# Pre-norm attention layer on one core: who issues the c transfers, and how finely the first output tile waits

## The chip, the core and the metric

The kernel runs on one core of a Trainium2 chip. The core has TensorE (PE, products), VectorE (DVE), ScalarE (ACT), GpSimd (POOL) and the sync engine (SP). Each runs its own instructions in order and waits for the others by semaphores; SP only waits and issues transfers. The metric is the device time of one execution in microseconds, lower is better.

## The reference

For each of 16 graphs of 512 nodes with 512 features: layer norm without weights, ReLU, 16-head attention under the adjacency mask, output projection and residual.

```
h = jnp.maximum(_layernorm(x, axis=-1), 0.0)
q = heads(h @ Wq + bq); k = heads(h @ Wk + bk); v = heads(h @ Wv + bv)
scores = jnp.einsum('bhqd,bhkd->bhqk', q, k) * scale
scores = jnp.where(mask[:, None] == 0, -jnp.inf, scores)
attn = jax.nn.softmax(scores, axis=-1)
x = x + (attn @ v) @ Wo + bo
```

## The kernel before

**Tiling.** A batch is one graph. The 16 heads go in four head groups g of four heads j. Queries and keys go in tiles of 128. Every projection is made of three products with operands split into a high and a low part (`w_hi`, `w_lo`, `hT_hi`, `hT_lo`, `oT_hi`, `oT_lo`), on four pieces kt of the inner dimension; an output tile's piece kt is head group kt of `oT`.

**Blocks and slots.** The program is a chain of blocks k = 0 to 17 with 64 slots u each, written out by `step(k, parity)` on every engine. Constants at the top fix the slot of everything. In slot u PE makes one score product of pass 1 (L797), one of pass 2 (L811, for some heads with a mask product L814), one kt of a projection tile T = u // 4 (L700 to L702), and in every fourth slot a value product into `psO` (L831). Block k projects q, k, v of batch k, and in its first 16 slots the four output tiles of batch k - 2 (`TILES`); pass 1 of a batch starts at slot 35, pass 2 at slot 60.

**The two passes.** Pass 1 computes the scores with queries on partitions. DVE adds the mask and takes the row maximum (L592), ScalarE takes the exponential and its sum (L430). After a head group DVE forms c from maximum and log-sum (`form_c`, L528 to L533), in a high and a low part. PE turns them (L758), DVE copies them to `c_rows` (L551; slots 8, 24, 40 and 56 for groups 1, 2, 3 and, of the next batch, 0), and two transfers (`load_c`, L388) put them into two extra rows of `q_stack`. Pass 2 computes the scores again, transposed and with c as part of the product, so its exponential (L470) is the softmax itself; for six of eight heads DVE masks it (L599). The first product of pass 2 of a head group waits for `c_in`; the groups start at slots 60, 12, 28 and 44.

**Stacks.** The q and k tiles leave PSUM as a high part (ScalarE, L454) and a low part (DVE, L634) and go by 12 transfers a tile into `q_stack` and `k_stack` (`load_stack`, L223, in the pieces hi0, lo, hi1 of four transfers each).

**The output.** `psO` of a head group leaves as `oT_hi` (ScalarE, L444) and `oT_lo` (DVE, L613); group 3 of batch k - 2 does so in slot 63 of block k - 1, right before block k begins with output tile 0. GpSimd adds bo to a y tile (L343, it waits for the tile's load, L265), DVE adds the output tile (L626), SP stores it (L272). In the last batch GpSimd's adds also wait for the last `c_parts`.

**Queues.** SP issues in this order within a slot: x, adjacency, store of y, load of y, stack. Nothing behind a waiting SP instruction goes out before it. The c transfers are issued by ScalarE, one slot after DVE's copy. In SP's queue load_y for slots 44 and 46 follows the k and q stacks; in the block after the last batch's projections it has no stack before it. PE keeps three banks for pass 1 (`bank1`, `wait_bank1`) and two for projections. `due(n)` is n, at least 0; `have(b)` is true for an existing batch.

## Time and profile before

| | us |
|---|---|
| median of 3 runs | 1709.16 |
| lowest, highest | 1708.68, 1709.55 |
| the profiled execution | 1711.46 |
| its span, first to last instruction | 1709.7 |
| PE busy | 1655.3 (97%) |
| DVE busy | 1527.0 (89%) |
| ACT busy | 1477.9 (86%) |
| POOL busy | 153.1 (9%) |

### The profile page before, as it was taken

The page shows a single profiled execution, that of the slowest core. Times are in us where ns is not written, and L with a number is a line of the kernel's source. Part 1 is how long each engine was busy: PE and PEld are TensorE (multiplying, and loading weights), DVE is VectorE, ACT ScalarE, POOL GpSimd, SP SyncE. Part 2 cuts the span into 40 slices and gives each one's busy share as a digit, 9 for nine tenths or more (in the row PEclk, how much of TensorE's full clock was granted, in tenths as well). Part 3 has the DMA queues.
Part 4 walks back from the last instruction along what each step waited for, and adds up shares of the span by engine and source line. Part 5 has one row for each costly group of instructions (what it writes and reads, how often), then busy time and mean ns, then how long its engine had stood idle before and what let it go on. Part 6 is the DMA issues. An engine that isn't in the chain of part 4 may idle for free.

```text
span 1709.7 us, 27479 instructions
## 1 busy us (share of the span) xinstructions
PE 1655.3 (97%) x7876; PEld 1035.4 (61%) x8001; DVE 1527.0 (89%) x3656; ACT 1477.9 (86%) x3498; POOL 153.1 (9%) x203
## 2 busy tenths in 40 slices
PE   6899999999999999999999999999999999999997
PEld 5556666666666666666665666666666666666653
DVE  4799998989989899998999989899998999989895
ACT  3799898898888989899898988989899888989985
POOL 2001100001010011100011000111100001000001
PEclk9799999999999999999999999999999999999998
DMA  6433343333433334343333433344343433433320
GB/s 198 107 86 100 106 111 90 113 90 110 116 95 108 88 113 109 100 108 89 114 92 109 114 92 106 93 118 111 102 106 86 112 96 106 114 97 94 92 85 26
DMA packets 117166, 175.18 MB, mean 102 GB/s; under 512 B 30860, under 2 KB 32920, under 8 KB 117016
## 3 DMA queue, kind: packets, MB, share of 16 engines
q1 hardware_dynamic: 112536, 171.83, 37.3%
q10 hardware_dynamic: 4480, 1.58, 0.4%
q8 instruction: 66, 1.08, 0.3%
q14 instruction: 84, 0.69, 0.1%
HBM read 54.79 MB, written 16.78 MB: 42 GB/s over the span
## 4 chain that ended last, share of the span: by engine, by line
PE 78%; DVE 15%; issue 3%; ACT 2%; SPq 1%; DMA 0%; DVEq 0%; ACTq 0%
PE ps L797 14%; PE psO L831 13%; PE psP L700 13%; PE psP L701 11%; PE ps L811 11%; PE psP L702 11%; DVE ps L592 5%; DVE probs L599 4%; PE ps L814 2%; PE ps L747 1%; DVE x_tile L513 1%; DVE stats L505 1%; ACT ps L430 1%; DVE y_tile L626 1%; DVE oT_lo L613 1%
## 5 line engine op out<-in xcount | busy, mean ns | idle before, releaser
L592 DVE CUSTOM_DVE_ANT_0 ps<-ps,bias_q 128x512 f32<-128x512 f32 x1024 | 708.7, 694 | 132.5 <-PE ps L797 122.4
L430 ACT ACTIVATE ps<-ps,neg_max 128x512 f32<-128x512 f32 x1024 | 686.9, 671 | 92.1 <-DVE neg_max L592 75.6
L470 ACT ACTIVATE probs<-ps 128x512 f32<-128x512 f32 x1024 | 622.5, 608 | 72.0 <-PE ps L814 37.7
L599 DVE SCALAR_TENSOR_TENSOR probs<-bias_k,probs 128x512 f32<-128x512 bf16 x768 | 552.9, 721 | 8.2 <-ACT probs L470 8.1
L797 PE MATMUL ps<-k_stack,q_stack 96*128 96x512 f32 x1024 | 450.8, 441 | 21.3 <-ACT ps L430 11.5
L811 PE MATMUL ps<-q_stack,k_stack 98*128 98x512 f32 x1024 | 410.0, 401 | 3.2 <-ACT probs L470 3.0
L797 PEld LDWEIGHTS ps<-k_stack,q_stack 96*128 96x128 f32 x1024 | 193.6, 189 | 277.0 <-ACT ps L430 132.2
L831 PE MATMUL psO<-probs,v_sb 128*32 128x512 f32 x2048 | 274.5, 608 | 2.0 <-DVE oT_lo L613 0.9
L811 PEld LDWEIGHTS ps<-q_stack,k_stack 98*128 98x128 f32 x1024 | 194.9, 190 | 40.1 <-ACT probs L470 14.9
L430 ACT ACTIVATION_READ_ACCUMULATOR ps<-ps,neg_max 128x1 f32 x1024 | 218.2, 213 | 0.0
L592 DVE DVE_READ_ACCUMULATOR2_ANT neg_max<- 128x1 f32 x1024 | 144.0, 141 | 0.0
L343 POOL TENSOR_TENSOR y_tile<-y_tile,bo_row 128x512 f32<-128x512 f32 x62 | 84.8, 1367 | 412.0 <-DMA y_tile<-in_x_dram 384.7
L700 PE MATMUL psP<-wo_hi,oT_hi 128*128 128x512 f32 x248 | 111.8, 451 | 9.3 <-DVE oT_lo L613 9.3
L329 POOL TENSOR_SCALAR mean_var<-mean_var 128x1 f32<-128x1 f32 x64 | 20.7, 323 | 1108.5 <-DVE mean_var L508 1108.4
L700 PE MATMUL psP<-wv_hi,hT_hi 128*128 128x512 f32 x256 | 114.1, 446 | 0.8 <-DVE hT_lo L544 0.8
L700 PE MATMUL psP<-hT_hi,wq_hi 128*128 128x512 f32 x256 | 114.4, 447 | 0.2 <-DVE hT_lo L544 0.2
L700 PE MATMUL psP<-hT_hi,wk_hi 128*128 128x512 f32 x256 | 113.2, 442 | 0.4 <-DVE wk_lo L556 0.3
L701 PE MATMUL psP<-hT_lo,wq_hi 128*128 128x512 f32 x256 | 102.8, 402 | 0.0
L701 PE MATMUL psP<-wv_lo,hT_hi 128*128 128x512 f32 x256 | 102.2, 399 | 0.0
L702 PE MATMUL psP<-hT_hi,wq_lo 128*128 128x512 f32 x256 | 102.0, 399 | 0.0
L702 PE MATMUL psP<-wv_hi,hT_lo 128*128 128x512 f32 x256 | 101.7, 397 | 0.0
L701 PE MATMUL psP<-hT_lo,wk_hi 128*128 128x512 f32 x256 | 101.6, 397 | 0.0
(75 smaller groups left out, 1882.2 us busy)
## 6 DMA issues: line engine op xcount, KB each, us to landing
q_stack<-part_hi SPq DMA_DIRECT2D x512, 64.0 KB, 2.0
k_stack<-part_hi SPq DMA_DIRECT2D x504, 64.0 KB, 2.0
x_tile<-in_x_dram SPq DMA_DIRECT2D x64, 256.0 KB, 2.9
y_tile<-in_x_dram SPq DMA_DIRECT2D x64, 256.0 KB, 2.9
adj_tile<-in_adj_dram SPq DMA_DIRECT2D x64, 256.0 KB, 3.0
q_stack<-part_lo SPq DMA_DIRECT2D x256, 64.0 KB, 2.0
k_stack<-part_lo SPq DMA_DIRECT2D x256, 64.0 KB, 2.0
out_dram<-y_tile SPq DMA_DIRECT2D x62, 256.0 KB, 2.1
```

The costliest lines, as they stand in the source:

```text
L343: nc.gpsimd.tensor_tensor(y_view(b, t), y_view(b, t), bo_row[:], ALU.add).then_inc(y_plus_bo, 1)
L430: nc.scalar.activation(item, item, ACT.Exp, scale=-1.0, bias=neg_max[:, g % 2, col:col + 1], accum_out=exp_sum[:, col:col + 1]).then_inc(e ...
L470: nc.scalar.activation(probs[:, n % P_RING, :], ps2[:, n % 2, :], ACT.Exp, scale=SCALE).then_inc(exp2_done, 1)
L592: nc.vector.tensor_tensor_reduce(bank1(("s", u)), bank1(("s", u)), bias_q[:, qt, :], -SCALE, 3.0e38, ALU.add, ALU.min, neg_max[:, g % 2, c ...
L599: nc.vector.scalar_tensor_tensor(out=probs[:, n % P_RING, :], in0=bias_k[:, n % 16 // 4, :], scalar=-MASKED, in1=probs[:, n % P_RING, :], ...
L700: nc.tensor.matmul(acc, w_h, m_h, start=(kt == 0), stop=False)
L701: nc.tensor.matmul(acc, w_h, m_l, start=False, stop=False)
L702: return nc.tensor.matmul(acc, w_l, m_h, start=False, stop=(kt == NT - 1))
L797: nc.tensor.matmul(bank1(("s", u)), q_stack[0:STACK, g, j, P * qt:P * qt + P], k_stack[0:STACK, g, j, :], start=True, stop=True).then_inc( ...
L811: last = nc.tensor.matmul(ps2[:, n % 2, :], k_stack[:, g, j, P * kt:P * kt + P], q_stack[:, g, j, :], start=True, stop=(n % 8 in VECTOR_MA ...
L814: last = nc.tensor.matmul(ps2[:, n % 2, :], ident_b[:], bias_k[:, kt, :], start=False, stop=True)
L831: last = nc.tensor.matmul(psO[32 * j:32 * j + 32, :], v_sb[:, 1 - parity, kt, at:at + DH], probs[:, (4 * n + j) % P_RING, :], start=(kt == ...
```

## The change

The c transfers go from ScalarE's queue to SP's, but for the first pair of all. In SP's order they stand in slot 9 (group 1, after the store of an output tile), slot 25 (group 2, after an adjacency load and before a k stack), slot 37 (group 3, inside the k stack, after its pieces hi0 and lo) and slot 57 (group 0). The first output tile's wait for all four head groups of `oT` becomes one wait before each kt, for that group.

```diff
--- before.py
+++ after.py
@@ -223,6 +223,14 @@
                     queue.dma_start(stack[row:row + 32, g, j, :].bitcast(F32),
                                     part[32 * j:32 * j + 32, i % 2, :].bitcast(F32)).then_inc(stack_in[kind], 16)
 
+        def load_c(queue, b, g):
+
+            if have(b):
+                queue.wait_ge(c_rows_done, due(4 * b + g + 1))
+                for part in range(2):
+                    queue.dma_start(q_stack[STACK + part:STACK + part + 1, g, :, :].rearrange("a j (t q) -> a (j t) q", q=P).bitcast(F32),
+                                    c_rows[16 * part:16 * part + 16, :].bitcast(F32)).then_inc(c_in, 16)
+
         def halves(b, g):
 
             return [slice(0, S // 2), slice(S // 2, S)] if (b, g) == (LAST, NT - 1) else [slice(0, S)]
@@ -288,10 +296,20 @@
                     if u in (7, 11) and k - 2 != LAST: load_y(k - 2, (u + 1) // 4)
                     if u in (44, 46): load_y(k - 1, (u - 44) // 2)
                     if u in (48, 50) and k - 1 == LAST: load_y(LAST, (u - 44) // 2)
+                    if u == 9: load_c(sp, k - 1, 1)
+                    if u == 25: load_c(sp, k - 1, 2)
+                    if u == 57 and k > 0: load_c(sp, k, 0)
+                    if u == 37 and not tile_at(k, 8): load_c(sp, k - 1, 3)
                     if u % 4 == 1:
                         done = tile_at(k, u // 4 - 1) if u >= 4 else tile_at(k - 1, 15)
                         if done and done[0] in "qk" and done != ("k", 0, 0):
-                            load_stack(sp, done[2], QK_ORDER.index(done[:2]))
+                            i = QK_ORDER.index(done[:2])
+                            if u == 37:
+                                load_stack(sp, done[2], i, ("hi0", "lo"))
+                                load_c(sp, k - 1, 3)
+                                load_stack(sp, done[2], i, ("hi1",))
+                            else:
+                                load_stack(sp, done[2], i)
                         if done == ("k", 0, 0):
                             load_stack(sp, 0, QK_ORDER.index(("k", 0)), ("lo",))
 
@@ -379,14 +397,6 @@
                 kind, n = QK_ORDER[i]
                 if have(k):
                     act.wait_ge(stack_in[kind], due(192 * (4 * k + n + 1)))
-
-            def load_c(b, g):
-
-                if have(b):
-                    act.wait_ge(c_rows_done, due(4 * b + g + 1))
-                    for part in range(2):
-                        act.dma_start(q_stack[STACK + part:STACK + part + 1, g, :, :].rearrange("a j (t q) -> a (j t) q", q=P).bitcast(F32),
-                                      c_rows[16 * part:16 * part + 16, :].bitcast(F32)).then_inc(c_in, 16)
 
             nc.scalar.preload_act_table_set("natural_log_exp_and_others")
 
@@ -471,7 +481,7 @@
                                              ).then_inc(exp2_done, 1)
                     for kind, n, rel in TURNS.get(u - 1, ()):
                         if kind == "c":
-                            load_c(k + rel, n)
+                            if (k + rel, n) == (0, 0): load_c(act, 0, 0)
                     for kind, n, rel in TURNS.get(u, ()):
                         if kind == "h" and have(k):
                             act.wait_ge(h_turned, due(4 * k + n + 1))
@@ -709,10 +719,6 @@
                 if kt == 0:
 
                     wait_tile_out(*((k, T - 2) if T >= 2 else (k - 1, T + 14)))
-                    if T == 0:
-
-                        pe.wait_ge(o_hi_done, due(4 * b + 4))
-                        pe.wait_ge(o_lo_done, due(4 * b + 4))
                     if T == 4 or k == 0 and kind == "v":
 
                         pe.wait_ge(h_hi_done, due(4 * b + (4 if T == 4 else n + 1)))
@@ -721,6 +727,10 @@
                         pe.wait_ge(w_lo_done[kind], 1)
                 if k == 0 and n == 0 and kind == "v":
                     pe.wait_ge(w_lo_done["v"], kt + 1)
+                if T == 0 and kind == "o":
+
+                    pe.wait_ge(o_hi_done, due(4 * b + kt + 1))
+                    pe.wait_ge(o_lo_done, due(4 * b + kt + 1))
                 acc = psP[:, T % 2, :]
                 rows = slice(P * n, P * n + P)
                 if kind in "qk":
```

On PE, the start of a block: output tile 0. First before:

```order
L797 MATMUL ps<-k_stack,q_stack 128x512 [waits exp1_done]
L811 MATMUL ps<-q_stack,k_stack 128x512 [waits exp2_done,m_done]
L700 MATMUL psP<-wo_hi,oT_hi 128x512 [waits o_hi_done,o_lo_done,qk_lo_done,qk_hi_done]
L701 MATMUL psP<-wo_lo,oT_hi 128x512
L702 MATMUL psP<-wo_hi,oT_lo 128x512
L797 MATMUL ps<-k_stack,q_stack 128x512 [waits exp1_done]
L811 MATMUL ps<-q_stack,k_stack 128x512 [waits exp2_done]
L700 MATMUL psP<-wo_hi,oT_hi 128x512
L701 MATMUL psP<-wo_lo,oT_hi 128x512
```

and now:

```order
L807 MATMUL ps<-k_stack,q_stack 128x512 [waits exp1_done]
L821 MATMUL ps<-q_stack,k_stack 128x512 [waits exp2_done,m_done]
L710 MATMUL psP<-wo_hi,oT_hi 128x512 [waits o_hi_done,o_lo_done,qk_lo_done,qk_hi_done]
L711 MATMUL psP<-wo_lo,oT_hi 128x512
L712 MATMUL psP<-wo_hi,oT_lo 128x512
L807 MATMUL ps<-k_stack,q_stack 128x512 [waits exp1_done]
L821 MATMUL ps<-q_stack,k_stack 128x512 [waits exp2_done]
L710 MATMUL psP<-wo_hi,oT_hi 128x512 [waits o_lo_done,o_hi_done]
L711 MATMUL psP<-wo_lo,oT_hi 128x512
```

The wait for `o_hi_done` and `o_lo_done` stands before each product L710 of the tile, each with a count of its own (L700 and L710, L797 and L807 are the same lines).

On SP, slots 24 to 25 of a block. Before:

```order
L223 DMA q_stack<-part_hi 32x512 [waits qk_hi_done]
L223 DMA q_stack<-part_hi 32x512 x3
L252 DMA adj_tile<-in_adj_dram 128x512 [waits bias_done]
L223 DMA k_stack<-part_hi 32x512 [waits qk_hi_done,scores2]
L223 DMA k_stack<-part_hi 32x512 x3
L223 DMA k_stack<-part_lo 32x512 [waits qk_lo_done]
L223 DMA k_stack<-part_lo 32x512 x3
```

and now:

```order
L223 DMA q_stack<-part_hi 32x512 [waits qk_hi_done]
L223 DMA q_stack<-part_hi 32x512 x3
L260 DMA adj_tile<-in_adj_dram 128x512 [waits bias_done]
L231 DMA q_stack<-c_rows 1x16x128 [waits c_rows_done]
L231 DMA q_stack<-c_rows 1x16x128
L223 DMA k_stack<-part_hi 32x512 [waits qk_hi_done,scores2]
L223 DMA k_stack<-part_hi 32x512 x3
L223 DMA k_stack<-part_lo 32x512 [waits qk_lo_done]
L223 DMA k_stack<-part_lo 32x512 x3
```

The pair of c stands between the adjacency load and the k stack, and all that follows is two issues later.

On SP, slots 37 to 44. Before:

```order
L223 DMA k_stack<-part_lo 32x512 [waits qk_lo_done]
L223 DMA k_stack<-part_lo 32x512 x3
L223 DMA k_stack<-part_hi 32x512 [waits qk_hi_done]
L223 DMA k_stack<-part_hi 32x512 x3
L265 DMA y_tile<-in_x_dram 128x512 [waits y_out0]
L223 DMA q_stack<-part_hi 32x512 [waits qk_hi_done,scores2]
```

and now:

```order
L223 DMA k_stack<-part_lo 32x512 [waits qk_lo_done]
L223 DMA k_stack<-part_lo 32x512 x3
L231 DMA q_stack<-c_rows 1x16x128 [waits c_rows_done]
L231 DMA q_stack<-c_rows 1x16x128
L223 DMA k_stack<-part_hi 32x512 [waits qk_hi_done,scores2]
L223 DMA k_stack<-part_hi 32x512 x3
L273 DMA y_tile<-in_x_dram 128x512 [waits y_out0]
L223 DMA q_stack<-part_hi 32x512 [waits qk_hi_done,scores2]
```

The pair waits in the middle of the k stack, and the load of y comes behind it.

On SP, the end of the program, from the last batch's c on. Before:

```order
L272 DMA out_dram<-y_tile 128x512 [waits y_done]
L265 DMA y_tile<-in_x_dram 128x512 [waits y_out1]
L272 DMA out_dram<-y_tile 128x512 [waits y_done] x2
L265 DMA y_tile<-in_x_dram 128x512 [waits y_out0]
L265 DMA y_tile<-in_x_dram 128x512 [waits y_out1]
L265 DMA x_tile<-in_x_dram 128x512 [waits h_turned] x2
L272 DMA out_dram<-y_tile 128x512 [waits y_done] x2
```

and now:

```order
L231 DMA q_stack<-c_rows 1x16x128 [waits c_rows_done]
L231 DMA q_stack<-c_rows 1x16x128
L273 DMA y_tile<-in_x_dram 128x512 [waits y_out1]
L280 DMA out_dram<-y_tile 128x512 [waits y_done] x2
L231 DMA q_stack<-c_rows 1x16x128 [waits c_rows_done]
L231 DMA q_stack<-c_rows 1x16x128
L231 DMA q_stack<-c_rows 1x16x128 [waits c_rows_done]
L231 DMA q_stack<-c_rows 1x16x128
L273 DMA y_tile<-in_x_dram 128x512 [waits y_out0]
L273 DMA y_tile<-in_x_dram 128x512 [waits y_out1]
L273 DMA x_tile<-in_x_dram 128x512 [waits h_turned] x2
L280 DMA out_dram<-y_tile 128x512 [waits y_done] x2
```

The four loads of the last y tiles (two of them into `x_tile`) now follow the last pair of c.

## Rows read from the trace of the kernel before

**Rows 1.** Page: busy time by engine; shares of the chain that ended last.

```profile
PE 1655.3 (97%) x7876; PEld 1035.4 (61%) x8001; DVE 1527.0 (89%) x3656; ACT 1477.9 (86%) x3498; POOL 153.1 (9%) x203
...
PE 78%; DVE 15%; issue 3%; ACT 2%; SPq 1%; DMA 0%; DVEq 0%; ACTq 0%
```

**Rows 2.** What PE waited for: us in total, times, longest us.

```profile
PE psP L700 <- DVE oT_lo L613: 9.3, 16, 1.2
```

**Rows 3.** Order of time, a block's first slots: start us, us, engine, line, operation.

```profile
798.26 0.40 PE L797 MATMUL ps<-k_stack,q_stack 96*128 96x512 f32 x1
...
798.49 0.39 PE L811 MATMUL ps<-q_stack,k_stack 98*128 98x512 f32 x1
798.53 0.74 DVE L613 SCALAR_TENSOR_TENSOR oT_lo<-psO,cols,oT_hi 128x512 fp32r<-128x512 f32 x1
...
799.42 0.47 PE L700 MATMUL psP<-wo_hi,oT_hi 128*128 128x512 f32 x1 [0.53 <-DVE oT_lo L613]
...
800.19 0.40 PE L797 MATMUL ps<-k_stack,q_stack 96*128 96x512 f32 x1
...
800.62 0.70 DVE L592 CUSTOM_DVE_ANT_0 ps<-ps,bias_q 128x512 f32<-128x512 f32 x1 [0.69 <-PE ps L797]
...
800.71 0.27 ACT L430 ACTIVATION_READ_ACCUMULATOR ps<-ps,neg_max 128x1 f32 x1
```

**Rows 4.** Order of time, ScalarE, slots 57 and 58 of a block.

```profile
787.38 0.51 ACTq L388 DMA_DIRECT2D q_stack<-c_rows  x1
...
787.93 0.61 ACTq L388 DMA_DIRECT2D q_stack<-c_rows  x1
...
788.59 0.66 ACT L430 ACTIVATE ps<-ps,neg_max 128x512 f32<-128x512 f32 x1 [0.25 <-issue]
```

**Rows 5.** Line 388, the c transfers: who waited (us, times), landing times.

```profile
  PEld ps L811: 0.6, 2
...
DMA to landing us min/median/max: 1.8/1.9/3.4
```

**Rows 6.** Order of time, the sync queue, around slot 25.

```profile
1252.83 0.59 SPq L252 DMA_DIRECT2D adj_tile<-in_adj_dram  x1
1253.51 2.41 SPq L223 DMA_DIRECT2D k_stack<-part_hi  x4
```

**Rows 7.** k_stack transfers issued from 1253.4 to 1254.3: landing times.

```profile
DMA to landing us min/median/max: 2.4/2.4/2.5
```

**Rows 8.** Order of time, PE, slot 28 of the same block.

```profile
1256.32 0.40 PE L811 MATMUL ps<-q_stack,k_stack 98*128 98x512 f32 x1
```

**Rows 9.** Order of time, the sync queue, slots 40 to 44.

```profile
865.60 2.49 SPq L223 DMA_DIRECT2D k_stack<-part_hi  x4
868.13 0.58 SPq L265 DMA_DIRECT2D y_tile<-in_x_dram  x1
```

**Rows 10.** Order of time, GpSimd, slots 46 to 52 of that block.

```profile
871.18 1.62 POOL L343 TENSOR_TENSOR y_tile<-y_tile,bo_row 128x512 f32<-128x512 f32 x1 [2.28 <-DMA y_tile<-in_x_dram]
880.68 1.30 POOL L343 TENSOR_TENSOR y_tile<-y_tile,bo_row 128x512 f32<-128x512 f32 x1 [7.88 <-DMA y_tile<-in_x_dram]
```

**Rows 11.** Order of time, DVE, the same slots.

```profile
872.82 0.69 DVE L599 SCALAR_TENSOR_TENSOR probs<-bias_k,probs 128x512 f32<-128x512 bf16 x1
...
880.85 1.68 DVE L599 SCALAR_TENSOR_TENSOR probs<-bias_k,probs 128x512 f32<-128x512 bf16 x1
```

**Rows 12.** Windows, slots 40 to 56 of two blocks: length, then busy us by engine.

```profile
1379.50:1400.50 21.00, 20.56 (x102) 12.94 (x101) 20.31 (x49) 18.33 (x46) 4.17 (x6) 1.00 0.44 111
1071.10:1091.20 20.10, 20.10 (x101) 13.04 (x101) 19.41 (x50) 18.71 (x45) 4.60 (x6) 1.00 0.46 114
```

**Rows 13.** Order of time, GpSimd, in the last block.

```profile
1673.62 2.98 POOL L343 TENSOR_TENSOR y_tile<-y_tile,bo_row 128x512 f32<-128x512 f32 x2 [27.37 <-DVE c_parts L533]
```

**Rows 14.** Order of time, DVE, in the last block.

```profile
1678.76 0.27 DVE L551 CAST c_rows<-ps 32x128 fp32r<-32x128 f32 x1
...
1683.63 2.00 DVE L599 SCALAR_TENSOR_TENSOR probs<-bias_k,probs 128x512 f32<-128x512 bf16 x3 [1.17 <-ACT probs L470]
1685.93 0.75 DVE L613 SCALAR_TENSOR_TENSOR oT_lo<-psO,cols,oT_hi 128x512 fp32r<-128x512 f32 x1 [0.30 <-ACT oT_hi L444]
```

## Prediction

> **What bounds the kernel now.** I read the page first: TensorE (PE) is busy 97% of the span and holds 78% of the chain that ended last, VectorE (DVE) 15% [rows 1]. PE is near its own pace, so only two things move the time: PE stalls that go and PE stalls that come. I read the list of what PE waited for, then the order of time around each place that the diff touches.
>
> The first place is the first output tile of a block. The list has 16 waits of its first product for `oT_lo`, 9.3 us together, the longest 1.2 [rows 2]; 15 are this tile (the output tiles of batches 0 to 14) and the longest is the one at the end, which the change leaves alone. In the order of time PE starts one product 0.23 us after another (798.26, 798.49), but the first output product comes 0.93 us after the one before it, when DVE has written `oT_lo` [rows 3]. So the stall is 0.93 - 0.23 = 0.70 us of PE's pace, and 0.53 in the idle column only because the ends of products are modelled.
>
> The second place is the scalar queue. A pair of c transfers takes 0.51 + 0.61 us of issue there, and the exponential behind it starts 0.25 us late [rows 4]. PE hardly waits for these transfers: two waits, 0.6 us in all, of 64 pairs, both at the end of the kernel [rows 5].
>
> **The sum, part by part**, made against the profiled execution (span 1709.7, time 1711.46, of which 1.8 lie around the span and stay). The median of the runs shown is 1709.16, 2.3 lower; the forecast is for such a median, so the sum is put on 1709.16.
>
> *Waits per head group: -10.3 us.* At kt 0, 1 and 2 the products need head groups that were ready long before; only kt 3 needs the late one, and before it stands the value product of slot 2, which waits for the same `oT_lo`. PE gets there about two slots later, while DVE ends `oT_lo` at 798.53 + 0.74 = 799.27 [rows 3], so the wait is over. What is late next? The score product now at 800.19 moves to 799.49 and needs a bank whose exponential is done by then; the one after it moves to about 801.0 and needs the exponential that ends at 800.71 + 0.27 = 800.98 [rows 3]. Both just fit; I take off 0.02 to 0.1. DVE follows: before its next reduction it idles 0.69 us waiting for that very product [rows 3], so DVE, which is full over the next ten slots, also starts 0.7 earlier and does not take the gain back. 15 x 0.69 = 10.3; bounds 9 and 10.8 (0.6 and 0.72 a batch).
>
> *Issues taken from ScalarE: -0.3 us.* 63 of 64 pairs go, 63 x 1.12 = 71 us of issue. In the steady part the late exponential is covered: PE has three score banks, keeps starting products at its pace and DVE is behind anyway. Only in the last block, where ScalarE is on the chain for some slots, do two pairs count; 0 to 1 us, I take 0.3.
>
> *c for head group 2 behind the adjacency load: +1.7 us.* In the sync (SP) queue the pair comes behind a whole q stack and an adjacency load. In a typical batch that load is issued at 1252.83 and the first k piece at 1253.51 [rows 6]. The c pair takes the place of the first two k pieces, so its second transfer goes out at about 1254.1. Alone it would land 1.9 us later [rows 5], at 1256.0; the two k pieces that stand there now land after 2.4 us [rows 7], which gives 1256.5. The product that needs c starts at 1256.32 [rows 8]. So 0.3 us early by one row and 0.2 late by the other. I take 0.11 a batch, nearer to the k pieces, as they are in the same queue behind the same load, but are larger: 15 x 0.11 = 1.7; bounds 0 and 0.23 x 15 = 3.5, since any lateness here is straight on PE's path. So a transfer right behind this load lands 0.5 us later than one on the other queue. The Trainium skill ("DMA: Bandwidth & Descriptors", Queues, rings and completion order) says that scalar and sync queue own a ring each on the same engines, that an engine takes turns between rings but works through one ring in order. The trace agrees so far as the 2.4 shows. The rule speaks against the change: by it the pair lands with the load's data, like the k pieces, and the term is near 3.5 rather than 0.
>
> *c for head groups 1 and 3 and 0: +0.8 us.* Group 0 is issued into an idle SP queue, earlier than now. Group 3 stands after eight pieces of a k stack, about when its rows are ready. Group 1 must now follow the wait for an output tile and its store. Landings scatter by 1.6 us (1.8 to 3.4 [rows 5]), so a few may be late; group 1 is followed by slots in which PE waits for DVE anyway, which covers most of it. 0 to 3, I take 0.8.
>
> *The y load behind the k stack: +5 us.* All that is queued behind the pair moves back. The adjacency load after the k stack of group 2 has slack. But at slot 37 the pair sits inside a k stack, and behind it, with no gap, comes the load of a y tile (the last four pieces at 865.60, the load at 868.13 [rows 9]); it goes out 0.51 + 0.61 us [rows 4] to 1.25 us (two of the pieces, four of which take 2.49 [rows 9]) later, say 1.2, and so does GpSimd's add of bo, which waits for it (now 871.18 [rows 10]). That add and DVE's masking step (L599) exclude each other: where the add at 880.68 [rows 10] runs, the mask started at 880.85 takes 1.68 us and ends 0.55 after the add, where none runs (872.82) it takes 0.69 [rows 11]. Today the first add falls on steps of DVE that do not care. At 871.18 + 1.2 = 872.4 it runs until 873.7, and the mask at 872.82 must wait: 873.7 + 0.55 - 873.5 = 0.7 us lost. How much reaches PE? In a batch where both adds hit (masks 1.1 and 0.6 us too long) the stretch has 21.00 - 20.56 = 0.44 us of PE idle (0.9 by the starts of its products, an estimate), in one where only the second hit, none [rows 12]. So DVE has some 0.65 us to spare, and the second add uses that up already. Placed against the start of slot 46, the first add begins in 11 of the 15 blocks, that of [rows 10] among them, where 1.2 us later is worse by some 0.6, and in four, that of the first stretch of [rows 12] among them, where it is better (there it hits now) by some 0.4; both are my estimates from the same reckoning. 11 x 0.6 - 4 x 0.4 = 5; bounds 0 and 8. The Trainium skill ("SBUF — State Buffer", SBUF: two separate sides) states such a lock between the two engines for a step with two SBUF inputs; the trace agrees (1.68 against 0.69).
>
> *The end: +2.5 us.* The last batch's four y loads stand in SP's queue behind the last c pair. Now they are long there and GpSimd adds at 1673.62, as soon as `c_parts` is done [rows 13], in slots where PE has other work. After, they go out only when the c rows are copied (1678.76 + 0.27 [rows 14]) and the pair is issued: 1680.2, landing by about 1683.2, and four adds run until about 1690. In that time the masks of the last heads start at 1683.63 (three in 2.00 us) and `oT_lo` at 1685.93 [rows 14]. Each mask would wait for an add, one in about 1.7 us (two take 2.98, the first of them 1.3 as in [rows 10]): three end at 1688.5 instead of 1685.63, `oT_lo` is 2.5 us late, and PE's next output product waits for it. Bounds 1 and 3.5.
>
> Sum: -10.3 - 0.3 + 1.7 + 0.8 + 5 + 2.5 = -0.6. From 1709.16: **1708.6 us**.
>
> **The rivals.**
> *The gain stays* (faster). For it: the removed stall is read directly, 15 times; the y load's new place depends on when loads land, and 0.5 us less would put the add where it costs nothing. Against: the adds that do hit. With the 5 as 0, c of group 2 at 0.5 and the other groups at 0.6: -10.3 - 0.3 + 0.5 + 0.6 + 2.5 = -7.0, 1702.
> *The adds hit the masks* (slower). The same mechanism as in the sum, behind the y load of slot 44, at its full price: the first add makes a mask 1.1 us too long in every block, the second 0.6, together 1.7, less the spare 0.65 about 1.05, where the blocks lose some 0.3 today: 15 x 0.75 = 11 instead of 5, and c of group 2 at 3.5 instead of 1.7. -0.6 + 6 + 1.8 = +7.2, 1716. It decides when the new stalls of the blocks pass (10.3 + 0.3 - 2.5 + 3.4) / 15 = 0.77 us each; the sum has (1.7 + 0.8 + 5) / 15 = 0.5. For it speaks that the add's place is set by a landing time, against it that a block in which the add is free exists for every delay.
> *The head-group wait only moves* (slower or same). If the score product two further on must wait for the exponential that I put 0.02 us ahead of it, a part of the 0.7 stays: at a gain of 0.3 a block, 4.5 in place of 10.3, the sum is +5.2, 1714. The rows leave little room for it, since DVE's idle 0.69 goes too.
>
> **How the numbers follow.** A measurement of this kernel can tell 0.2%, 3.4 us. Likeliest is that gain and new stalls balance: 0.43, within 3.4 us of 1709.2. Gain stays: 0.34. Adds at full price: 0.16; wait moves: 0.07. Faster 0.34, same 0.43, slower 0.23. The likeliest case alone spans 1705.8 to 1712.5; the range takes in most of the first rival and part of the second: 1701 to 1714.
>
> **What would show it.** Right: the wait of the first output product for `oT_lo` gone from PE's list but for the one at the end; DMA issues of c under SP; GpSimd's first add about 1.2 us later after slot 46, with masks of over 1.2 us there; the last four adds around 1683 to 1690 instead of 1673 to 1680; PE waits for `q_stack<-c_rows` at group 2. Wrong: a wait of equal size at the score product of slot 1 or 2; or a y load that lands where no mask stands, with the time some 7 us down.

## The result

Over 22 runs each the changed kernel takes 1712.9 us at the median (1709.1 to 1718.8), the kernel before 1710.3: **ratio 1.0018, 95% interval 1.0010 to 1.0026**. The forecast was 1708.6, that is 0.03% faster. So it is slower by about 3 us. The median lies inside the range of 1701 to 1714 and 0.4 us above the 1705.8 to 1712.5 of the likeliest case, and the interval leaves out both "no change" and "faster". The unedited changed kernel, run again beside some of the experiments on another chip, gave 0.9997 (0.9984 to 1.0011), which can't be told from no change. Both comparisons weighted by their widths put the change at +0.13%, 2.1 us, and that is what the steps are held against below.

The profiled execution of the changed kernel has a span of 1710.4 us. Its page, busy time by engine and the shares of the chain that ended last (compare [rows 1]):

```profile
PE 1659.1 (97%) x7876; PEld 1035.2 (61%) x8001; DVE 1530.9 (90%) x3656; ACT 1471.2 (86%) x3498; POOL 153.1 (9%) x203
...
PE 73%; DVE 15%; issue 4%; ACT 4%; SPq 2%; DMA 1%; another core or an unknown queue 0%; DVEq 0%; ACTq 0%
```

The page hardly differs. The list of what PE waited for does (us in total, times, longest us; compare [rows 2]):

```profile
PE psP L710 <- DVE oT_lo L623: 3.6, 2, 2.4
PE ps L821 <- DMA q_stack<-c_rows: 2.2, 4, 0.9
```

Sixteen waits for `oT_lo` have become two: the one of 1.2 us that was always at the end, and a new one of 2.4. And PE now waits for c. The product that follows the wait of [rows 3] stood 0.93 us behind its predecessor; in the same block of the changed kernel, PE's order of time (start us, us, engine, line, operation):

```profile
795.99 0.40 PE L821 MATMUL ps<-q_stack,k_stack 98*128 98x512 f32 x1
...
796.22 0.40 PE L710 MATMUL psP<-wo_hi,oT_hi 128*128 128x512 f32 x1
```

It now comes 0.23 us behind. So the stall that the change aimed at is gone, and the time came back elsewhere. To see where, I cut the traces at PE's score products of pass 1, four slots at a time, and summed each stretch over blocks 1 to 15. Worked out from those starts, changed kernel less the kernel before, in us (first and second profiled execution):

| stretch | 1st | 2nd | forecast |
|---|---|---|---|
| slots 0 to 3, 15 blocks | -9.5 | -9.4 | -10.3 with block 16 |
| slots 28 to 31 | +2.9 | +2.0 | +1.7 |
| slots 48 to 55 | +5.5 | +8.2 | +5 |
| slots 12 to 15 | -0.3 | +1.9 | part of +0.8 |
| slots 44 to 47 and 60 to 63 | 0 | +0.2 | part of +0.8 |
| all other slots of blocks 1 to 15 | -0.5 | -0.8 | 0 |
| ahead of block 1 | -1.1 | -1.5 | 0 |
| block 16, up to the last score product of pass 1 | +1.1 | +2.0 | part of -10.3 |
| behind that product (the tail) | +2.6 | +0.1 | +2.5 |
| sum (span) | +0.8 | +2.7 | |

Of block 16, -0.2 is the wait. Most of the rest comes in the slots in which TensorE is granted half its clock (1.2 GHz) for 3.4 us (first profile, from 1648.0) and for 6.8 us (second). Before's profile has no such stretch there; eight of the 14 profiles of the study have one, that of "delay only" below among them, which moves neither c nor the waits. Ahead of block 1 every other profile is shorter than before's too, by 0.3 to 2.0 us, so that row says nothing of the change.

### The profile page after: what moved, and what is told of

It reads as the page before. It is cut to its first block, busy times and chain, and to the rows that moved or that the text cites. A ratio compares the mean times of both kernels' runs of the same rounds, so it can differ in the third digit from the quotient of the medians.

```text
span 1710.4 us, 27540 instructions
## 1 busy us (share of the span) xinstructions
PE 1659.1 (97%) x7876; PEld 1035.2 (61%) x8001; DVE 1530.9 (90%) x3656; ACT 1471.2 (86%) x3498; POOL 153.1 (9%) x203
## 4 chain that ended last, share of the span: by engine, by line
PE 73%; DVE 15%; issue 4%; ACT 4%; SPq 2%; DMA 1%; another core or an unknown queue 0%; DVEq 0%; ACTq 0%
PE ps L807 14%; PE psO L841 12%; PE psP L710 12%; PE ps L821 11%; PE psP L711 11%; PE psP L712 10%; DVE ps L602 5%; DVE probs L609 4%; ACT ps L440 2%; PE ps L824 1%; SPq L223 1%; PE ps L757 1%; DVE x_tile L523 1%; ACT probs L480 1%; DVE stats L515 1%
## 5 line engine op out<-in xcount | busy, mean ns | idle before, releaser
L807 PE MATMUL ps<-k_stack,q_stack 96*128 96x512 f32 x1024 | 451.6, 441 | 21.4 <-ACT ps L440 11.5
L807 PEld LDWEIGHTS ps<-k_stack,q_stack 96*128 96x128 f32 x1024 | 194.0, 189 | 280.2 <-ACT ps L440 113.7
L440 ACT ACTIVATION_READ_ACCUMULATOR ps<-ps,neg_max 128x1 f32 x1024 | 222.7, 217 | 0.0
L710 PE MATMUL psP<-wo_hi,oT_hi 128*128 128x512 f32 x248 | 111.9, 451 | 3.6 <-DVE oT_lo L623 3.6
L710 PE MATMUL psP<-wv_hi,hT_hi 128*128 128x512 f32 x256 | 113.7, 444 | 0.9 <-DVE hT_lo L554 0.8
L710 PE MATMUL psP<-hT_hi,wq_hi 128*128 128x512 f32 x256 | 114.0, 445 | 0.2 <-DVE hT_lo L554 0.2
L710 PE MATMUL psP<-hT_hi,wk_hi 128*128 128x512 f32 x256 | 113.3, 443 | 0.3 <-DVE wk_lo L566 0.3
```

Source lines behind the costliest of these rows:

```text
L440: nc.scalar.activation(item, item, ACT.Exp, scale=-1.0, bias=neg_max[:, g % 2, col:col + 1], accum_out=exp_sum[:, col:col + 1]).then_inc(e ...
L710: nc.tensor.matmul(acc, w_h, m_h, start=(kt == 0), stop=False)
L807: nc.tensor.matmul(bank1(("s", u)), q_stack[0:STACK, g, j, P * qt:P * qt + P], k_stack[0:STACK, g, j, :], start=True, stop=True).then_inc( ...
```

## The experiments

Where a run is called so many us faster or slower than the kernel before, that is its ratio less 1, times 1711; the changed kernel counts as 2.1 us slower. With 6 to 12 runs of each kernel such a figure is good to 2 to 4 us. The table at the end has the stretches of all of them, each from one profile.

### The two halves of the change alone

```diff
 # kernel before, c on the scalar queue
-                    if T == 0:
-                        pe.wait_ge(o_hi_done, due(4 * b + 4))
-                        pe.wait_ge(o_lo_done, due(4 * b + 4))
...
+                if T == 0 and kind == "o":
+                    pe.wait_ge(o_hi_done, due(4 * b + kt + 1))
+                    pe.wait_ge(o_lo_done, due(4 * b + kt + 1))
```

> One part of the change alone: the first output tile waits per head group, and all c pairs stay on the scalar queue. Theory 'ledger' (the wait's gain is cancelled by costs of the c transfers on the sync queue): the stretch of slots 0 to 3 is 9.5 us shorter over the 15 blocks in the changed kernel's trace and nothing else moves here, so 9.5 us faster than the kernel before, ratio 0.9944 (0.9935 to 0.9955). The tensor engine's waits for DVE's oT_lo at a block's start are gone, and the stretch of slots 48 to 55 has its old length. Rival 'idle time moves' (the tensor engine comes earlier to the next group of slots and waits there for ScalarE or for a mask, so the gain is handed back whatever queue carries c): ratio 0.999 to 1.001, with the other groups of slots longer by 9 us in sum.

Measured 0.993 (0.9910 to 0.9951), 12 us faster. The rival falls: slots 0 to 3 are 9.0 us shorter, and the other stretches take back 2.4 at most (slots 12 to 15 and 48 to 55).

```diff
 # changed kernel, the two edits of the wait undone
-                if T == 0 and kind == "o":
-                    pe.wait_ge(o_hi_done, due(4 * b + kt + 1))
-                    pe.wait_ge(o_lo_done, due(4 * b + kt + 1))
...
+                    if T == 0:
+                        pe.wait_ge(o_hi_done, due(4 * b + 4))
+                        pe.wait_ge(o_lo_done, due(4 * b + 4))
```

> The other part alone: all c pairs but the first on the sync queue, the old wait at slot 0 kept. Ledger: +2.9 us at slots 28 to 31, +5.5 us at slots 48 to 55, +2.6 us in the tail, together 11 us slower than the kernel before, ratio 1.0064; up to 1.0075 if the further stretch at half clock in the last block (1.6 us) comes with it. Rival 'not additive' (the later c pairs and y loads are late only because the block starts 0.65 us earlier, so without the new wait they hit nothing): ratio 1.000 to 1.003.

Measured 1.0061 (1.0042 to 1.0080), 10 us slower, with +3.9 in slots 28 to 31 and +6.2 in slots 48 to 55. The rival "not additive" falls. The halves add up to -2 us, within some 5 us by their intervals, so they agree with the whole (+2.1); the change is a gain and a loss of about one size, not two edits that do nothing.

### The changed kernel once more

> The changed kernel once more, unedited, so that its variants stand beside it on one chip, and for a second profiled execution of it. The sums by groups of slots should repeat: slots 0 to 3 shorter by 9.0 to 9.5 us over the 15 blocks, slots 28 to 31 longer by 2.9 us, slots 48 to 55 by 5.5 us (4 to 7). The stretches of TensorE at half clock in the last block and the tail (five in the first profiled execution, 1648 us on) are the open point. Theory 'the clock comes with the kernel': four or five stretches again, a tail behind the last score product of 43 us, ratio 1.001 to 1.003. Rival 'the clock is drawn by lot': three stretches or fewer, a tail of 39 to 41.5 us, and the same ratio all the same, since the sum over many executions holds both.

Ratio 0.9997; sums in the table above. It has three stretches at half clock in the last block and the tail instead of five, and a tail of 40.5 us. That is what the second theory, the lot, said; the one stretch that does come with the kernel is looked at under "The end".

### Head group 3's pair, and the y load behind it

```diff
 # changed kernel; group 3's pair issued by the scalar queue
-                    if u == 37 and not tile_at(k, 8): load_c(sp, k - 1, 3)
...
-                                load_stack(sp, done[2], i, ("hi0", "lo"))
-                                load_c(sp, k - 1, 3)
-                                load_stack(sp, done[2], i, ("hi1",))
+                                load_stack(sp, done[2], i)
```

> The changed kernel with head group 3's pair back on the scalar queue and the k stack of slot 37 issued in one piece again; the other groups stay on the sync queue. Ledger: y loads of slots 44 and 46 go out 1.2 us earlier again, the GpSimd adds end before DVE's masks, slots 48 to 55 lose 5.5 us, and the last batch's y loads stand behind one pair less, which gives back up to 2.6 us in the tail: 6 to 8 us faster than the changed kernel, so 3.5 to 5.5 us faster than the kernel before, ratio 0.997 to 0.998. Rival 'the adds are not the cause' (slots 48 to 55 grew because the block's start moved against the ScalarE or because of the k stack's last piece): slots 48 to 55 keep at least 4 of the 5.5 us and the ratio is 1.000 to 1.002.

Measured 0.9959 (0.9943 to 0.9975), 7 us faster than before and 9 faster than the changed kernel. That is more than the 3.5 to 5.5 us expected, though slots 48 to 55 keep +3.0 of 5.5 to 8.2, where the theory had nothing left and the rival at least 4. The difference lies in the tail, which has its shortest length, 36.7. Slots 28 to 31, with group 2's pair still on the sync queue, keep +2.8.

The opposite test puts only the delay into the kernel before:

```diff
 # kernel before; pad is a tile that nobody reads, c stays on the scalar queue
+                            if u == 37 and k > 0:
+                                load_stack(sp, done[2], i, ("hi0", "lo"))
+                                sp.wait_ge(pad_in, 32 * (k - 1))
+                                for part in range(2):
+                                    sp.dma_start(pad[16 * part:16 * part + 16, :], ident[16 * part:16 * part + 16, :]).then_inc(pad_in, 16)
+                                load_stack(sp, done[2], i, ("hi1",))
```

> The kernel before, with nothing of the change: only two small transfers (8 KB each, into a tile that nobody reads) on the sync queue at the place in the k stack of slot 37 where the changed kernel has its c pair. It tests the delay of the y loads by itself, with c on the scalar queue and the old waits. Theory 'the adds meet the masks': the first GpSimd add starts at slot 46 plus 0.9 to 2 us instead of slot 45/46 plus 0.9 us, slots 48 to 55 grow by 5 to 8 us over the 15 blocks (5.5 and 8.2 in the two profiles of the changed kernel) and nothing else does; ratio 1.003 to 1.005. Rival 'the delay is harmless, what costs is c's own lateness': slots 48 to 55 within 1.5 us of the kernel before, ratio 0.999 to 1.001.

Measured 1.0029 (1.0014 to 1.0043), 5 us slower. Two transfers that nobody waits for cost time, because of what stands behind them. The sync queue of this kernel, then GpSimd and DVE some 3 us later, in order of time:

```profile
1077.30 1.22 SPq L301 DMA_DIRECT2D pad<-ident  x2
1078.62 2.44 SPq L225 DMA_DIRECT2D k_stack<-part_hi  x4
1081.10 0.58 SPq L267 DMA_DIRECT2D y_tile<-in_x_dram  x1
```

```profile
1084.15 1.27 POOL L353 TENSOR_TENSOR y_tile<-y_tile,bo_row 128x512 f32<-128x512 f32 x1 [3.44 <-DMA y_tile<-in_x_dram]
1092.61 1.35 POOL L353 TENSOR_TENSOR y_tile<-y_tile,bo_row 128x512 f32<-128x512 f32 x1 [7.19 <-DMA y_tile<-in_x_dram]
```

```profile
1084.04 0.69 DVE L602 CUSTOM_DVE_ANT_0 ps<-ps,bias_q 128x512 f32<-128x512 f32 x1
...
1084.64 1.33 DVE L609 SCALAR_TENSOR_TENSOR probs<-bias_k,probs 128x512 f32<-128x512 bf16 x1
```

The y load goes out at 1081.10, the add runs from 1084.15 to 1085.42, and the mask that starts in it (1084.64) ends 0.55 after it: 1.33 us instead of 0.69. The reduction at 1084.04, which reads PSUM, overlaps the add and keeps its 0.69. Slots 48 to 55 grow by 3.2, less than the 5 to 8 expected. Slots 12 to 15, which the edit doesn't touch, grew by 5.3 in this profile. I have no reason for that: the masks of slots 6 to 15 are lengthened by adds as much as before (11.9 us in all against 12.1, worked out as in the next paragraph). So a stretch of a single profile is good to a few us only.

The masks of all 14 profiles show the lock and its price. Each profile has over 700 masks that no add overlaps, and none of them takes more than 0.70 us; the 53 to 65 that an add overlaps take 0.9 to 1.2 in the median and up to 1.83. What the masks of slots 46 to 55 take above 0.70 us each, summed over 15 blocks, follows the place of the y loads: 5.5 to 9.0 us in the five kernels with the loads in their old place (5.8 before), 10.3 to 14.7 in the seven that delay them (14.7 and 13.4 in the changed kernel, 11.4 here), and nothing in the two kernels below that load y early. The first add starts 0.37 us after the start of slot 46 before (median of the blocks), 1.34 and 1.69 in the changed kernel, and 1.39 here.

The third test leaves every pair where the change has it and moves the y loads:

```diff
 # changed kernel
-                    if u in (44, 46): load_y(k - 1, (u - 44) // 2)
+                    if u in (44, 46) and k - 1 == LAST: load_y(k - 1, (u - 44) // 2)
+                    if u == 36 and k - 1 != LAST:
+                        for t in range(2): load_y(k - 1, t)
```

> The changed kernel with the y loads of slots 44 and 46 issued at slot 36, ahead of the k stack and its c pair; nothing taken back. Theory 'the adds meet the masks' (the y load behind the c pair makes the GpSimd add start 1.2 us later, which lengthens DVE's masks and so the scores): the adds start at slot 44 or 45, slots 48 to 51 give back their 3.1 us, slots 52 to 55 at least 1.5 of their 2.4 us unless the first add's new place stretches another mask, in sum 3 to 5.5 us faster than the changed kernel, ratio 0.9985 to 1.0000. Rival 'it is the score products of slots 48 to 55 that wait for stacks, not for masks': ratio and slots as in the changed kernel (1.0018, +5.5 us). Rival 'the add just moves onto another mask': slots 40 to 47 grow by what slots 48 to 55 lose, ratio 1.001 to 1.002.

Ratio 1.0006 (0.9995 to 1.0016): nothing won, and none of the three theories has it right. Slots 48 to 55 are 3.6 us shorter than even before, their masks free of adds. But slots 44 to 47 grew by 7.8, and not through a mask. The sync queue, and PE's weight load of the product that needs the pair:

```profile
1474.85 0.58 SPq L260 DMA_DIRECT2D adj_tile<-in_adj_dram  x1
1475.47 0.93 SPq L273 DMA_DIRECT2D y_tile<-in_x_dram  x2
1476.50 2.41 SPq L223 DMA_DIRECT2D k_stack<-part_hi  x4
```

```profile
1485.84 0.19 PEld L823 LDWEIGHTS ps<-q_stack,k_stack 98*128 98x128 f32 x1 [1.58 <-DMA q_stack<-c_rows]
```

From slot 33 on the queue has no gap, so two loads put in ahead make group 3's pair, whose margin in the first profile of the changed kernel was 0.4 to 1.6 us, late for 13 of 16 batches (PE's weight loads waited 28 times for c, 18.4 us, against 10 times and 5.4 us). A part of the 3.6 us can be DVE and ScalarE catching up while PE waited for c, for without that wait the same move shortens slots 48 to 55 by less. With c on the scalar queue the move is free:

```diff
 # kernel with the waits alone
-                    if u in (44, 46): load_y(k - 1, (u - 44) // 2)
+                    if u in (44, 46) and k - 1 == LAST: load_y(k - 1, (u - 44) // 2)
+                    if u == 36 and k - 1 != LAST:
+                        for t in range(2): load_y(k - 1, t)
```

> The waits per head group with all c pairs on the scalar queue (as in the run of that part alone, ratio 0.993), and the y loads of slots 44 and 46 issued at slot 36. If the adds that meet masks also cost the kernel before something: slots 48 to 55 take 196.2 us in it over 15 blocks, and without any lengthened mask 4 x 6.11 x ... is not known, so bounded by the wait lists: the blocks with the least take 12.3 us for the eight slots, which gives 185 us for 15, so up to 4 us more than the first part alone can be had, ratio 0.991 to 0.993. Rival 'the add moves onto another mask': 0.993 to 0.995.

Measured 0.9944 (0.9930 to 0.9958). Slots 48 to 55 are at -0.2, slots 44 to 47 at 0. That is 1.7 us better in the profile than the waits alone, and not to be told from it by the ratios. It is also hardly better than the kernel before, whose masks were 5.8 us longer; unless the moved waits cost something there, so much lengthening costs PE little.

### Head group 2's pair

```diff
 # changed kernel; group 2's pair issued by the scalar queue
-                    if u == 25: load_c(sp, k - 1, 2)
```

> The changed kernel with head group 2's pair back on the scalar queue, so that it is not behind the adj load and the q stack on the sync queue. Theory 'the queue makes it late': slots 28 to 31 go back to 6.11 us a block, 2.9 us in all, the tensor engine's waits for that pair go (longest margin again 1.9 us), 2.9 us faster than the changed kernel, ratio to the kernel before about 1.000. Rival 'the pair is not what is late' (it is the q stack ahead of it that a slow issue holds up, whoever carries the pair): slots 28 to 31 keep 2 us or more, ratio 1.0013 to 1.0018.

Measured 0.9991 (0.9975 to 1.0007), 1.5 us faster than before and 3.6 faster than the changed kernel; slots 28 to 31 are back at 6.11 us in every block. So the pair is what was late, and the rival falls. The second test keeps it on the sync queue and changes what is ahead of it:

```diff
 # changed kernel; ADJ_AT[1] is slot 24, where its load is taken out
+                    if u == 25:
+                        load_c(sp, k - 1, 2)
+                        load_adj(k, 1)
```

> The changed kernel with the adj load of slot 24 issued behind head group 2's pair instead of ahead of it; all pairs stay on the sync queue. Theory 'the term of head group 2 is the queue ahead of it': the pair goes out 0.63 us earlier, its margin goes from 0.04 to 0.3 us to about 0.8 us, which covers all but the issues that take 1.2 us or more, so slots 28 to 31 give back 2 to 2.9 us over the 15 blocks, ratio 0.001 to 0.0015 below the changed kernel's. Rival 'the adj load is then what comes late' (DVE turns it into the mask bias two slots later): slots 28 to 39 grow by 1 us or more and nothing is won.

Measured 0.9981 (0.9966 to 0.9996). Slots 28 to 31: +0.2 instead of +2.0 to 2.9; slots 32 to 39 don't grow, so the adj load is not late. In the changed kernel the product came 0.04 to 0.23 us after its pair had landed (blocks 1 to 15), and 0.04 means that it had waited for it, as it did in five of the 15 blocks. Now the distance is about 1.0: the pair goes out 0.63 earlier and lands faster. Behind the load its second transfer mostly took 2.0 to 2.5 us to land, ahead of it 1.84 to 1.95. One pair of the changed kernel, then one of this kernel, from issue to landing:

```profile
DMA to landing us min/median/max: 2.2/2.3/2.4
```

```profile
DMA to landing us min/median/max: 1.8/1.8/1.8
```

The Trainium skill ("DMA: Bandwidth & Descriptors", Queues, rings and completion order) says that each of the engines works through one queue's ring in order; both numbers agree with it.

What the prediction missed is the shape of this loss. In 12 of the 15 blocks of the first profile the stretch is at most 0.13 us longer; three blocks hold 2.8 of the 2.9. The sync queue in one of them, and PE:

```profile
1449.70 2.49 SPq L223 DMA_DIRECT2D q_stack<-part_lo  x4
1452.23 3.60 SPq L223 DMA_DIRECT2D q_stack<-part_hi  x4
1455.88 0.58 SPq L260 DMA_DIRECT2D adj_tile<-in_adj_dram  x1
1456.50 1.15 SPq L231 DMA_DIRECT2D q_stack<-c_rows  x2
```

```profile
1459.33 0.50 PE L821 MATMUL ps<-q_stack,k_stack 98*128 98x512 f32 x1 [0.93 <-DMA q_stack<-c_rows]
```

Four issues take 2.49 us, these four 3.60, and everything behind them is 1.1 late. The kernel before has such issues too (34 of its 1536 stack issues take over 0.9 us, up to 2.2), one of them inside this row of its sync queue:

```profile
862.35 3.20 SPq L223 DMA_DIRECT2D k_stack<-part_lo  x4
```

There the stacks had slack for it, and c was on the other queue.

### The end

```diff
 # changed kernel
+                    if u in (44, 46) and k - 1 != LAST: load_y(k - 1, (u - 44) // 2)
+                    if u == 18 and k - 1 == LAST:
+                        for t in range(NT): load_y(LAST, t)
```

> The changed kernel, with one step moved: in the last block the four y loads are issued ahead of the last two c pairs (at slot 18) and no longer behind them. Ledger: the tail after the last score product is 2.6 us shorter, all else as in the changed kernel: 2.6 us faster than it, ratio to the kernel before 1.0000 (0.9993 to 1.0008). If the half-clock stretches in the last block go as well, 1.6 us more. Rival 'the clock makes the tail long' (the tail's growth is TensorE at half clock, which comes whatever the y loads do): the ratio stays at 1.0015 to 1.002 and the tail at 43 us.

Measured 0.9978 (0.9964 to 0.9991), 3.8 us faster than before and 5.9 faster than the changed kernel, where 2.6 was expected. The tail is 36.7 us instead of 43.0 and 40.5. In the changed kernel GpSimd, DVE and PE near its end:

```profile
1681.61 2.97 POOL L361 TENSOR_TENSOR y_tile<-y_tile,bo_row 128x512 f32<-128x512 f32 x2 [40.33 <-DMA y_tile<-in_x_dram]
1684.55 3.39 POOL L361 TENSOR_TENSOR x_tile<-x_tile,bo_row 128x512 f32<-128x512 f32 x2
```

```profile
1681.84 4.97 DVE L609 SCALAR_TENSOR_TENSOR probs<-bias_k,probs 128x512 f32<-128x512 bf16 x3 [1.46 <-ACT probs L480]
1686.73 0.74 DVE L623 SCALAR_TENSOR_TENSOR oT_lo<-psO,cols,oT_hi 128x512 fp32r<-128x512 f32 x1
```

```profile
1687.62 0.47 PE L710 MATMUL psP<-wo_hi,oT_hi 128*128 128x512 f32 x1 [2.42 <-DVE oT_lo L623]
```

Four adds from 1681.61 to 1687.94, three masks in 4.97 us instead of 2.00 [rows 14], and PE 2.42 us idle. Windows of the same stretch (length, busy us by engine, then TensorE's granted clock):

```profile
1685.20:1688.90 3.70, 1.28 (x9) 0.83 (x12) 3.70 (x4) 0.68 (x2) 2.74 (x2) 1.00 0.00 0
1688.90:1692.40 3.50, 3.50 (x12) 1.41 (x6) 0.88 (x2) 1.11 (x2) 0.00 (x0) 0.51 0.00 0
```

The windows of this experiment at the same distance (17.8 us on) from its last score product of pass 1; its adds ran from 1673.81:

```profile
1687.24:1690.94 3.70, 3.70 (x20) 1.85 (x19) 1.44 (x3) 1.90 (x4) 0.00 (x0) 1.00 0.00 0
1690.94:1694.44 3.50, 3.30 (x17) 1.44 (x16) 1.82 (x3) 1.94 (x4) 0.00 (x0) 1.00 0.02 5
```

From 1.3 us after the idle 2.42 us TensorE is granted 1.2 GHz for 3.4 us, and does 12 products; the other kernel, at 2.4 GHz throughout, does 17 in its window. Of six profiles with the late adds (both of the changed kernel and four experiments) all have the stall, 2.1 to 2.4 us; in four the clock falls 0.9 to 1.4 us after it, in one just before it ends, in one not. Of the eight with early adds none has the stall, and none a fall at that place. Their tails are 42.4 us in the mean (40.5 to 43.5) against 38.6 (36.7 to 41.1). So the end costs 3.8, not 2.5. Before's own tail, 40.4, is one of the long ones of its kind, which is why the first table has less. An idle stretch alone doesn't decide the clock: in before's profile PE is idle for 1.5 of the 4 us from 1648, and the clock stays.

### What a pair costs where nothing stands behind it, and both places mended

```diff
 # changed kernel; only group 0's pair (slot 57) stays on the sync queue
-                            if (k + rel, n) == (0, 0): load_c(act, 0, 0)
+                            if (k + rel, n) == (0, 0) or n == 1 or n == 2 or n == 3: load_c(act, k + rel, n)
```

> The waits per head group, with only head group 0's pair on the sync queue (it lands 3.4 us ahead of its need there, 2.1 us on the scalar queue) and the other three pairs back on the scalar queue. Theory 'a pair costs only what it pushes': at slot 57 nothing is queued close behind it, so the time is that of the waits alone, ratio 0.993 (0.991 to 0.995), slots 48 to 63 as in that run. Rival 'each pair on the sync queue costs a quarter of the loss' (12 us less for the waits, about 12 to 14 us back for four pairs): 3 us more, ratio 0.995 to 0.996, with slots 0 to 3 or 60 to 63 longer.

Measured 0.9939 (0.9916 to 0.9962), which can't be told from the time of the waits alone. Slots 48 to 63 are as in that run. A pair in a gap of the sync queue costs nothing that these runs can show.

```diff
 # changed kernel with both: group 3's pair on the scalar queue, adj behind group 2's
+                    if u == 25:
+                        load_c(sp, k - 1, 2)
+                        load_adj(k, 1)
...
+                            if (k + rel, n) == (0, 0) or n == 3: load_c(act, k + rel, n)
```

> The changed kernel with both costs of the sync queue taken away at once: head group 3's pair back on the scalar queue (k stack of slot 37 in one piece), and the adj load of slot 24 behind head group 2's pair. Groups 0, 1 and 2 stay on the sync queue, the waits per head group stay. Theory 'two places hold the whole loss' (the pair in the k stack with the y loads behind it, and the adj load ahead of group 2's pair): the gain of the waits stands alone, ratio 0.993 to 0.995; slots 28 to 31 and 48 to 55 together within 2.5 us of the kernel before, and the tail's adds start right behind the last slots. Rival 'the gain can't be had with pairs on the sync queue' (group 1's pair with its margin of 0.04 to 0.3 us is next, or issues on the sync queue get slower with it): ratio 0.996 or more, with slots 12 to 15 longer by 4 us or more.

Measured 0.9939 (0.9918 to 0.9960). With three of four pairs still on the sync queue the gain of the waits stands alone. So two places held the whole loss, to the 3.6 us that the interval allows: the pair inside the k stack, with the y loads behind it in the blocks and at the end, and the adj load ahead of group 2's pair. Four kernels (this one, "waits only", "y early, waits" and "group 0 sync", 0.9930 to 0.9944) can't be told apart; the simplest is the waits alone.

Stretches of all kernels in us against the kernel before (15 blocks each, worked out from the starts of PE's score products of pass 1), and the tail's own length. "Late" marks kernels whose last y loads stand behind the last c pair:

| kernel | 0-3 | 12-15 | 28-31 | 44-47 | 48-55 | tail | ratio |
|---|---|---|---|---|---|---|---|
| before | 0 | 0 | 0 | 0 | 0 | 40.4 | 1 |
| changed, 1st | -9.5 | -0.3 | +2.9 | 0 | +5.5 | 43.0 late | 1.0018 |
| changed, 2nd | -9.4 | +1.9 | +2.0 | +0.2 | +8.2 | 40.5 late | 0.9997 |
| waits only | -9.0 | +0.9 | 0 | 0 | +1.5 | 38.9 | 0.9930 |
| c on sync only | 0 | +1.4 | +3.9 | +1.2 | +6.2 | 41.4 late | 1.0061 |
| group 3 scalar | -9.0 | +3.9 | +2.8 | 0 | +3.0 | 36.7 | 0.9959 |
| last y first | -9.0 | 0 | +3.2 | 0 | +7.0 | 36.7 | 0.9978 |
| group 2 scalar | -9.4 | +2.5 | 0 | 0 | +2.1 | 42.9 late | 0.9991 |
| delay only | 0 | +5.3 | 0 | 0 | +3.2 | 41.1 | 1.0029 |
| y early, changed | -9.5 | -0.1 | +4.9 | +7.8 | -3.6 | 42.8 late | 1.0006 |
| y early, waits | -9.4 | +1.9 | 0 | 0 | -0.2 | 38.7 | 0.9944 |
| group 0 sync | -9.4 | +1.2 | 0 | 0 | +1.7 | 37.3 | 0.9939 |
| adj behind pair | -9.4 | +0.7 | +0.2 | 0 | +3.4 | 43.5 late | 0.9981 |
| both mended | -9.1 | +2.6 | 0 | 0 | +1.8 | 38.9 | 0.9939 |

## Why the prediction was wrong

The mechanisms were right, each at its place, and a balance near zero came out. But the sum said slightly faster and the kernel is slightly slower: -0.6 against +2.1 us. The steps that failed are three terms that were too kind: the count of the waits (by 0.6), the c pair of group 2 (by 0.8) and the end (by 1.3). A forecast of -0.6 from terms with bounds of several us could not tell the sign; that the sum came within 3 us is partly luck, since the term of the y load, the second largest, can't be pinned.

- **Waits per head group, -10.3: measured -9.7.** The price of one was right (0.67 of 0.69 us). The count was not: one of the 15 is in block 16, where ScalarE sets the pace, and gives back 0.21 only. 14 blocks make 9.5.
- **Issues taken from ScalarE, -0.3:** nothing to be seen of it. PE's longest list, score products that waited for exponentials, is 11.5 us before, 11.5 and 13.8 after.
- **Group 2's pair, +1.7: +2.0 and +2.9.** The place, the queue and the landing behind the load (2.4 forecast, mostly 2.0 to 2.5 measured) were right. The step that failed is "0.11 a batch": lateness was read from one typical batch of [rows 6]. A typical batch loses nothing, and a pair that is just punctual loses in the rare slow issues ahead of it, which only the spread of the issue times shows.
- **Groups 1, 3 and 0, +0.8:** near nothing. Group 1's product starts 0.04 to 0.33 us after its pair has landed, and in three or four blocks it waited; yet slots 12 to 15 have -0.3 to +3.9 us in the nine profiles with that pair on the sync queue and 0 to +5.3 in the five with it on the scalar queue.
- **The y load behind the k stack, +5: +5.5 and +8.2.** The mechanism is shown by the delay alone and by the masks of all profiles. The size can't be pinned: kernels that delay the load have +2.1 to +8.2, the four with the load in its old place and the waits moved have +1.5 to +3.0, though the profile of before, the base of it all, has 0. I take before's profile for a draw that is short by about 2.0, which makes the term 6.9 - 2.0 = 4.9. That is argued and not shown: all four have the waits moved, and an earlier start of the blocks could cost the 2.0 itself. Against that speaks that with the load delayed two kernels with the old wait have +3.2 and +6.2 and five profiles with the new one +2.1 to +8.2. That 4.9 meets the 5 is luck.
- **The end, +2.5: +3.8.** The stall was forecast at 2.5 and is 2.1 to 2.4. The step that failed is that it ends there: in four of the six profiles TensorE's clock falls behind it, in a fifth just before its end. That the stall brings the fall is what six profiles against eight suggest.

With these terms (2.5, 4.9 and 3.8 are means over profiles): -9.7 + 2.5 + 4.9 + 3.8 = +1.5, against +2.1. Of the rivals "the adds hit the masks at full price" fits the direction; its 11 us for the adds did not come. "The gain stays" did not come, since both profiles of the changed kernel have more adds in the masks; it takes an edit of both places (ratio 0.9939). "The wait only moves" is refuted by the waits alone.

Open: with group 2's pair punctual, slots 48 to 55 are longer by 2.1 and 3.4 us only, against 5.5 to 8.2 with it late. The ratios agree (5 us won by the adj load's move where slots 28 to 31 hold 2.5). Their masks are lengthened as much (13.9 and 11.2 us against 14.7 and 13.4), so less of it reaches PE. I have no reason for it that a run has tested. Nor is it known what makes an issue of the sync queue slow.

## What to carry to other kernels

Moving an issue to another queue cost nothing that could be measured where nothing follows it closely, and its full length to everyone behind it where the queue is dense; so list what stands behind the new place, and who waits for that, down to the last user. Where a transfer lands ahead of its need by less than one slow issue of its queue, take the spread of the issue times and not the median. And undo a change by halves before keeping or dropping it: here a gain of 0.7% was hidden under a loss of the same size.

## What the hardware showed beyond that

- Among steps of DVE, not only the masks with two SBUF inputs wait for a GpSimd add: the conversion of the adjacency tile did too, 1.52 us instead of 0.41 (it starts 0.41 into an add that ends at 871.67). In the 14 profiles 28 conversions overlap an add: 26 take 1.51 to 1.53, two 0.42; all others take 0.41 to 0.43. In the changed kernel:

```profile
870.03 1.64 POOL L361 TENSOR_TENSOR y_tile<-y_tile,bo_row 128x512 f32<-128x512 f32 x1 [4.10 <-DMA y_tile<-in_x_dram]
...
870.44 1.52 DVE L532 TENSOR_SCALAR bias_q<-adj_tile 128x512 bf16<-128x512 int32 x1
```

  The Trainium skill ("SBUF — State Buffer", SBUF: two separate sides) names DVE steps in a two-port mode or with two SBUF inputs as those that exclude a GpSimd step and are excluded by one; this step has one input, so it would have to be the former, which no row tells.
- A mask that starts while an add runs ends 0.55 us after that add, whenever it started: so 41 of 43 such masks in before's profile (the other two 0.64 and 0.67).
- An issue of a stack transfer on the sync queue takes 0.59 us in the median, but 34 to 42 of the 1536 of a profile take 0.9 to 2.2 us, in all 14 profiles, that of the kernel before included.
- Near the kernel's end a stall of TensorE of 2.1 to 2.4 us was followed, in four of six profiles, by 3.4 us at 1.2 GHz.
